# Graph network on one core: four transfers begun by GpSimd instead of ScalarE, and VectorE's gates, splits and low parts in another order

## The reference, cut to what matters

```python
for _ in range(5):
    s_in, s_out = state @ in_W.T + in_b, state @ out_W.T + out_b
    a = concatenate([A @ s_in, A.T @ s_out, state])
    r = sigmoid(a @ r_W.T + r_b)
    z = sigmoid(a @ z_W.T + z_b)
    h_hat = tanh(concatenate([a_in, a_out, r * state]) @ h_W.T + h_b)
    state = (1 - z) * state + z * h_hat
out = layernorm(x + tanh(state @ o1_W.T + o1_b) @ o2_W.T + o2_b)
```

## Time and profile before

| | us |
|---|---|
| median of 3 runs | 656.99 (656.04 to 657.47) |
| the profiled execution | 657.65 |
| its span, first to last instruction | 655.9 |
| mean granted TensorE clock | 0.996 |

### The profile page before, as it was taken

The page is one execution under the profiler, slowest core; times in us unless marked ns, Lnnn a source line. Parts: engine busy times, 40 slices in busy tenths (PEclk is TensorE's granted clock), DMA queues, the critical chain, the costliest instruction groups (busy, mean ns, idle before and its releaser), DMA issues. The chain is left out here.

```text
span 655.9 us, 8678 instructions
## 1 busy us (share of the span) xinstructions
PE 638.1 (97%) x2860; PEld 525.3 (80%) x2860; DVE 524.4 (80%) x833; ACT 418.2 (64%) x562; POOL 68.1 (10%) x61
## 2 busy tenths in 40 slices
PE   8999999999999999999999999999999999999993
PEld 7888888887888788788888877888887888887883
DVE  4996889799578739987896998887689888746886
ACT  2774645478357726895665688575758966674645
POOL 0092025200500720000000000000000000000012
PEclk9999999999999999999999999999999999999998
DMA  8999657213200270324034223403342250213003
GB/s 290 332 360 239 169 179 195 42 46 49 101 1 32 58 196 37 67 63 161 33 131 66 92 63 66 160 32 128 58 134 55 42 193 1 96 65 129 1 0 132
DMA packets 111609, 70.40 MB, mean 107 GB/s; under 512 B 89424, under 2 KB 95696, under 8 KB 110544
## 3 DMA queue, kind: packets, MB, share of 16 engines
q1 hardware_dynamic: 103056, 68.84, 35.1%
q10 hardware_dynamic: 8512, 1.05, 1.1%
HBM read 47.85 MB, written 19.40 MB: 103 GB/s over the span
## 5 line engine op out<-in xcount | busy, mean ns | idle before, releaser
L1158 ACT ACTIVATE work<-work,bias 128x512 f32<-128x512 f32 x120 | 86.0, 723 | 125.2 <-DVE work L1679 124.6
L1679 DVE SCALAR_TENSOR_TENSOR work<-degree,deg_w,bank 128x512 f32<-128x512 uint16 x120 | 88.4, 744 | 28.1 <-PE bank L703 27.3
L1017 ACT ACTIVATE ring<-a 128x1024 fp32r<-128x1024 uint8 (+1 forms) x91 | 91.7, 1048 | 6.3 <-PE bank L822 3.1
L701 PE MATMUL bank<-u_c,fold 128*128 128x512 f32 x240 | 94.1, 392 | 1.6 <-DVE work L1679 1.5
L702 PE MATMUL bank<-u_c,fold 128*128 128x512 f32 x240 | 93.4, 389 | 0.0
L703 PE MATMUL bank<-u_c,fold 128*128 128x512 f32 x240 | 93.4, 389 | 0.0
L822 PE MATMUL bank<-ring,rows 128*128 128x512 f32 x384 | 90.8, 390 | 0.3 <-DVE ring L1452 0.3
L714 PE MATMUL bank<-ring,rows 128*128 128x512 f32 x384 | 88.6, 389 | 0.2 <-issue 0.2
L1050 ACT ACTIVATE ring<-sums,minus 128x1024 fp32r<-128x1024 uint8 x72 | 80.3, 1139 | 7.5 <-PE bank L822 6.5
L822 PEld LDWEIGHTS bank<-ring,rows 128*128 128x128 f32 x384 | 71.7, 188 | 16.5 <-DVE ring L1452 1.0
L714 PEld LDWEIGHTS bank<-ring,rows 128*128 128x128 f32 x384 | 72.0, 188 | 15.5 <-issue 0.6
(11 more groups left out here) (168 smaller groups left out, 1110.9 us busy)
## 6 DMA issues: line engine op xcount, KB each, us to landing
sums<-sums_dram SPq DMA_DIRECT2D x12, 768.0 KB, 5.0
stage<-in_adj_dram SPq DMA_DIRECT2D x15, 512.0 KB, 8.6
sums<-in_adj_dram SPq DMA_DIRECT2D x13, 512.0 KB, 6.4
turned_dram<-work SPq DMA_DIRECT2D x12, 512.0 KB, 2.6
rows<-turned_dram SPq DMA_DIRECT2D x192, 32.0 KB, 2.0
sums_dram<-sums SPq DMA_DIRECT2D x4, 768.0 KB, 3.5
l_dram<-rs_c SPq DMA_DIRECT2D x3, 1024.0 KB, 3.9
rs_c<-l_dram SPq DMA_DIRECT2D x3, 1024.0 KB, 4.9
```

The lines of the kernel that those rows point to most:

```text
L701: nc.tensor.matmul(out_, wh, vh, start=first, stop=False)
L1017: nc.scalar.activation(out_, in_, ACT.Copy).then_inc(s, 1)
L1158: nc.scalar.activation(gates[:, g, e, :], gates[:, g, e, :], ACT.Tanh if g == H else ACT.Sigmoid, bias=bias[:, g, e:e + 1]).then_inc(gate_ ...
L1679: nc.vector.scalar_tensor_tensor(out=gates[:, g, e, :], in0=degree[:, c * CW:(c + 1) * CW], scalar=deg_w[:, g, e:e + 1], in1=g_bank[s % 3] ...
```

## The change

Six edits.

1. In the second chunk of a side VectorE reads gate 2 right behind gate 1, ahead of `rs(0)`, the turns, `rs_low(0)` and `rs(1)`. In the other chunks nothing moves.
2. For step 1 alone, the two `split_state` of each side leave the gate chunk before it and stand in `half_aggregate`, on ScalarE behind casts 13 and 15, on VectorE behind the first four tests of symmetry.
3. In `aggregate_pair`, side 0, the two `row_low(t, 1, h)` of VectorE stand behind the casts 2 and 3 and not ahead of them.
4. GpSimd's third `sum_blocks` waits for the mix W5 of the second side of step 1, and not for the states of the first.
5. The four transfers of chunk 3 that ScalarE began are begun by GpSimd, with a semaphore of their own (`rows_fourth`), for which every reader of these rows waits beside the old one.
6. The semaphore `zeroed` is folded into `const_ready`, whose last value is 9.

```diff
+            def turn_move(t):
+                k, n = NC - 1, NQ - 1
+                pool.wait_ge(turned, DB * NC * (t + 1))
+                for r in range(NQ):
+                    nc.gpsimd.dma_start(...).then_inc(rows_fourth, 16)
...
             pool.wait_ge(pair_stored, S_PAIR)
+            turn_move(0)
             pool.wait_ge(row_lo, row_count(1, (NC - 1, 1)))
             sum_blocks(1, range(6))
-            pool.wait_ge(state_new, S_TWO + 2 * TWO)
+            pool.wait_ge(mixed, mixed_at(1, 1, W5))
...
             sum_blocks(3, range(6))
+            for t in range(1, LAST):
+                turn_move(t)
...
@@ ScalarE, gate_chunk_two
-                if not ending:
+                if not ending and not half(t + (c == NC - 1)):
                     for e in range(DB):
                         split_state(*((t, 2) if c == 1 else (t + 1, 0)), e)
@@ ScalarE, half_aggregate
                 for k in range(10, 12):
                     if side == 0:
                         row_high(t, 2, k - 10)
-                        turn_move(t - 1, range(2 * (k - 10), 2 * (k - 9)))
                     cast(t, side, k)
                 for k in range(12, 16):
                     cast(t, side, k)
+                    if k % 2 == 1:
+                        split_state(t, 2 * side, k // 2 - 6)
@@ VectorE, gate_chunk
                     update(t, c - 1, first_gate=lambda: gate(t, c, 0))
                     next_pair(0)
                     gate(t, c, 1)
+                    gate(t, c, 2)
                     rs(t, c, 0)
...
-                gate(t, c, 2)
+                if not (c == NC - 1 or c == 1 and not first):
+                    gate(t, c, 2)
                 rs_low(t, c, 1)
...
-                if c == NC - 1 and not last or c == 1 and not first:
+                if (c == NC - 1 and not last or c == 1 and not first) and not half(t + (c == NC - 1)):
@@ VectorE, half_aggregate
                 for _ in range(4):
                     test()
+                for e in range(DB):
+                    split_state(t, 2 * side, e)
@@ VectorE, aggregate_pair
                 cast(t, side, 1)
                 if side == 0:
                     row_low(t, L1, 0)
-                    for h in range(2):
-                        row_low(t, 1, h)
...
                 cast(t, side, 3)
+                if side == 0:
+                    for h in range(2):
+                        row_low(t, 1, h)
```

More of the change, by code:

```diff
@@ L308, in fast_path @@
         fin_lo = sem("f_fin_lo")
-        zeroed = sem("f_zeroed")
         const_ready = sem("f_const_ready")
@@ L600, in _ @@
         def _(pool):
-            nc.gpsimd.memset(ident[:, :], 0.0).then_inc(zeroed, 1)
+            nc.gpsimd.memset(ident[:, :], 0.0).then_inc(const_ready, 1)
             nc.gpsimd.memset(ones[:, :], 1.0).then_inc(const_ready, 1)
@@ L608, in _ @@
                 nc.gpsimd.memset(minus[:, n:n + 1], -1.0 - n).then_inc(const_ready, 1)
-            pool.wait_ge(zeroed, 1)
+            pool.wait_ge(const_ready, 8)
             nc.gpsimd.affine_select(out=ident[:, :], in_=ident[:, :], compare_op=ALU.not_equal, fill=1.0,
@@ L630, in sum_bytes @@
                     n += level < len(TREE) - 1
+            def turn_move(t):
+                k, n = NC - 1, NQ - 1
+                pool.wait_ge(turned, DB * NC * (t + 1))
+                for r in range(NQ):
+                    nc.gpsimd.dma_start(rows[n * SQ:(n + 1) * SQ, LO, k * BC:(k + 1) * BC, :].bitcast(F32)
+                                        .rearrange("a b (e r d) -> a (b e) r d", e=DB, r=NQ)[:, :, r, :],
+                                        turned_T[r * SQ:(r + 1) * SQ, n].rearrange("p b e d -> p (b e) d")).then_inc(rows_fourth, 16)
             def sum_blocks(n_, some):
@@ L663, in _ @@
                 sum_bytes(c)
-            pool.wait_ge(const_ready, 8)
+            pool.wait_ge(const_ready, 9)
             pool.wait_ge(pair_ready, (NC - 1) * NP + 4)
@@ L987, in output @@
                         last.then_inc(o_done, 1)
-            pe.wait_ge(const_ready, 8)
+            pe.wait_ge(const_ready, 9)
             pe.wait_ge(ones_ready, 1)
@@ L1109, in split_state @@
                 high(st_c[:, HI, e, :], stateT[:, e, c * CW:(c + 1) * CW], st_hi)
[L1111 to L1119, removed]
             def row_high(t, k, h):
@@ L1144, in row_high @@
                     q, d = {L11: (2, 0), L21: (3, 0), L22: (3, 1)}[k]
-                    act.wait_ge(rows_loaded[q], 16 * NQ * NQ * t)
+                    if q == NC - 1:
+                        act.wait_ge(rows_fourth, 16 * NQ * t)
+                        act.wait_ge(rows_loaded[q], 16 * NQ * (NQ - 1) * t)
+                    else:
+                        act.wait_ge(rows_loaded[q], 16 * NQ * NQ * t)
                     high(rows[:, HI, q * BC:(q + 1) * BC, d * P:(d + 1) * P], rows[:, LO, q * BC:(q + 1) * BC, d * P:(d + 1) * P].bitcast(F32), row_hi)
@@ L1150, in row_high @@
                 else:
-                    act.wait_ge(rows_loaded[k], 16 * NQ * NQ * t)
+                    if k == NC - 1:
+                        act.wait_ge(rows_fourth, 16 * NQ * t)
+                        act.wait_ge(rows_loaded[k], 16 * NQ * (NQ - 1) * t)
+                    else:
+                        act.wait_ge(rows_loaded[k], 16 * NQ * NQ * t)
                     b = k * BC + 2 * h
@@ L1325, in aggregate_pair @@
                 cast(t, side, 8)
-                if side == 0:
-                    turn_move(t - 1, range(2))
                 cast(t, side, 9)
                 if side == 0:
-                    turn_move(t - 1, range(2, 4))
                     row_high(t, L1, 0)
@@ L1510, in l_add @@
                 if k == L2:
-                    dve.wait_ge(rows_loaded[3], 16 * NQ * NQ * t)
+                    dve.wait_ge(rows_fourth, 16 * NQ * t)
+                    dve.wait_ge(rows_loaded[3], 16 * NQ * (NQ - 1) * t)
                     dve.wait_ge(state_new, t * S_TWO)
```

3 lines of the change are left out of this document (2 added, 1 removed).

## The result

| | before | after |
|---|---|---|
| median, us | 657.12 (656.04 to 657.47, 4 runs) | 659.62 (659.42 to 660.28, 4 runs) |
| profiled execution, us | 657.65 | 659.42 |
| its span, us | 655.9 | 657.6 |
| mean granted clock | 0.996 | 0.995 |

Ratio of after to before: 1.0042, 95% interval 1.0027 to 1.0057. The change makes the kernel slower, by 1.8 to 3.7 us (the medians differ by 2.5, the ratio gives 2.8); 660.0 had been predicted, and slower with a chance of 0.80.

A forecast was written before the change was run, and what follows sets the result against it. TensorE, busy 638.1 of 655.9 us, was taken as the bound, with VectorE setting the end. Terms 1.5 + 1.4 + 2.4 - 0.6 - 1.2 - 0.7 = +2.8, rounded to 3: 656.99 + 3.0 = 660.0 us; 8-in-10 range 657.3 to 662.2.

The forecast's parts named there:

- A: Rival: fifth casts are in time, so early gate 2 costs only in the last chunk; 656.9 us, chance 0.12.
- B: Rival: reading gate 2 early frees TensorE and later work has slack enough; faster, 652.6 us, chance 0.08.
- C: Rival: the transfers begun by GpSimd are slow and readers wait; 668 us, or 664 if milder, chance 0.08.
- Part 1: Early gate 2, chunk 3 of steps 1 to 3: low part and fifth cast late, +0.5 us each, +1.5 us.
- Part 2: Early gate 2, chunk 1 of steps 2 to 4: fifth cast late, 0.45 us each, +1.4 us; step 1 free.
- Part 3: Early gate 2, last chunk of the last step: VectorE's queue stands still, gate 5 late, +2.4 us.
- Part 4: Splits out of the chunk before step 1's first side: fifth cast 0.6 us earlier, -0.6 us (ends 0 and -1.2).
- Part 5: GpSimd's third sum behind W5 in step 1: P5 casts no longer slowed, wait gone, -1.2 us.
- Part 6: Step 3, low parts behind casts 2 and 3: casts earlier, low parts with 0.2 us margin, -0.7 us.
- Part 7: Chunk 3's transfers begun by GpSimd: ScalarE's casts no earlier without them, no reader waits, 0 us.

The follow-up runs named there:

- e12: The changed kernel with VectorE's two low parts of the splits behind gate 5 in chunk 3 of steps 1 to 3; 657.67 us, ratio 1.0010.
- e9: e8 with gate 4 ahead of the two low parts of the split in chunk 3 of steps 1 to 3; 652.76 us, ratio 0.9935.
- e11: e8 with VectorE's two low parts of the splits behind gate 5 in chunk 3 of steps 1 to 3; 651.58 us, ratio 0.9919.
- e1: The changed kernel with gate 2 back in its old place behind rs(1) everywhere; 653.65 us, ratio 0.9943.
- e3: The kernel before with only gate 2 moved right behind gate 1 in the second chunk of each side; 664.15 us, ratio 1.0101.
- e2: The changed kernel with gate 2 in its old place in the last chunk of the last step alone; 657.40 us, ratio 1.0006.
- e7: The kernel before with only the splits of step 1's two sides moved into its aggregations; 655.58 us, ratio 0.9982.
- e6: The kernel before with only the low parts of row chunk 1 put behind casts 2 and 3; 655.81 us, ratio 0.9984.
- e10: e3 with chunk 3's four transfers begun by GpSimd instead of ScalarE, and `zeroed` folded into `const_ready`; 662.92 us, ratio 1.0094.
- e4: The changed kernel with chunk 3's four transfers begun by ScalarE again, on the new semaphore; 659.91 us, ratio 1.0041.
- e5: The kernel before with only GpSimd's third sum waiting for W5 of step 1's second side; 655.56 us, ratio 0.9984.
- e8: e1 with rs(1) and gate 2 ahead of rs_low(0) in chunk 3 of steps 0 to 3; 652.46 us, ratio 0.9929.

## Why the prediction was right, point by point

The predicted difference was +3.0 us; the ratio gives +2.8 (1.8 to 3.7). No rival came: A needed the fifth casts in time, B the low parts too, C slow transfers, and none of the three was so.

**Part 1 (+0.5 a chunk): right.** The wait for the low part took the place of the one for gate 2: 0.60, 0.48 and 0.44 us in steps 1 to 3 with the hidden 0.16, where 0.6 was predicted. From TensorE's first own matmul of h in chunk 2 to that in chunk 3 it took 16.96, 16.83 and 16.83 us where it had taken 17.00, 16.93 and 16.93, so the gain is 0.1 us or less. And the fifth cast was late: +0.56 and +0.55 in the two stretches where it stands alone. e12 shows that it is this cast. Its chain is gate 5, tanh, cast (e9, e11).

**Part 2 (+0.45 a chunk): right in size**, with +0.44, +0.47 and +0.63, but made of smaller pieces than I wrote; that they add up to the same is in part luck. I looked for one stall of 0.25 us of the matmuls. Steps 2 and 3 have none on the list of waits; only step 4 has (0.15 us of idle time). The weight loads show it. The weights are the rows, and the ring tile is the other factor, but TensorE's wait for the tile stands ahead of the load and the matmul alike, and so the load waits too, which elsewhere runs ahead of its matmul. In step 2 the fifth cast ends at 329.38 + 1.14 = 330.52, the load comes at 330.57, and from the second matmul of that tile on all are 0.11 us late, with 0.11 more at the next tile; some 0.1 more is lost at the own parts, whose low part is just in time.

```profile
329.38 2.18 ACT L1062 ACTIVATE ring<-sums,minus 128x1024 fp32r<-128x1024 uint8 x2
...
330.57 0.76 PEld L834 LDWEIGHTS bank<-ring,t_flat 128*128 128x128 f32 x4 [0.27 <-ACT ring L1062]
...
324.11 0.44 PE L713 MATMUL bank<-rs_c,own 128*128 128x512 f32 x1
```

Step 4 loses 0.2 more because I took step 2's rows for all three steps. In step 4 VectorE has a comparison of the symmetry test (L1621) between the second low part and gate 3, and everything behind it is later: the fifth cast ends at 565.47 + 1.14 = 566.61, which is 6.61 us behind the first own matmul (560.00), where it is 6.41 in step 2 (330.52 behind 324.11).

```profile
559.53 0.69 DVE L1621 SCALAR_TENSOR_TENSOR ident<-stage 128x512 uint8<-128x512 uint8 x1
...
565.47 2.18 ACT L1062 ACTIVATE ring<-sums,minus 128x1024 fp32r<-128x1024 uint8 x2
```

In step 1 chunk 1 costs 0.2 and not nothing (-1.06 against e1's -1.25), 0.11 of it at the own parts. That it is so little is owed to edit 2, which has taken the splits away: in e3, without edit 2, this stretch is 0.74 longer.

**Part 3 (+2.4): right**, +2.32, and e2 takes it away. The times counted through were 627.3 for ScalarE's last high parts, 629.2 for gate 3, 629.9 for the residual and 633.7 for gate 5; the trace has 627.33, 629.20, 629.86 and 633.56. A queue counted instruction by instruction, with each duration from a row, holds here to 0.15 us. That even the clock times agree is chance: the chunk begins where it did (its side's first own matmul of h at 603.63 us, before at 603.62), because gains and losses ahead of it had just cancelled.

**Part 4 (-0.6): right**, -0.55 with edit 1 and -1.20 without it (e1, e7): both of the numbers in its text, the value and the end of its range. The 0.65 between them is a cost of edit 1.

**Part 5 (-1.2): right**, -1.06 with edit 1, -1.27 alone. The P5 casts take 2.32 us for two where they took 4.29, since GpSimd's sum starts when they are over:

```profile
214.22 2.32 DVE L1460 TENSOR_TENSOR ring<-a 128x1024 fp32r<-128x1024 uint8 x2
...
219.35 1.42 POOL L656 TENSOR_TENSOR sums<-a,byte_one 128x512 uint32<-128x512 uint32 x1 [44.43 <-DVE work L1506]
```

**Part 6 (-0.7): right.** With part 1 in the same stretch -0.2 was forecast and -0.14 came; alone it is -0.68 (e6). In e1 it is -0.39. There the low parts begin 17.05 us behind TensorE's mark of the chunk and 16.73 in e6, and TensorE waits for them, since VectorE waited longer for the rows over DRAM (0.76 us, in e6 0.43). So the prediction's margin of 0.2 us was about right for the landing that it had read, and a later landing uses it up. What the prediction did not see is that parts 1 and 6 work on the same wait: e3 and e10, which have edit 1 and not edit 3, are no longer than before in this stretch (0.00 and -0.10), because TensorE, late by part 1, finds the P5 casts done. The sum of the two parts is right, but how much of it edit 3 brings in the changed kernel no run here tells: none takes edit 3 alone out of it.

```profile
391.09 0.69 DVE L1528 TENSOR_TENSOR work<-rows 128x512 f32<-128x512 f32 x1 [0.76 <-DMA rows<-turned_dram]
```

**Part 7 (0): the total right, the reason wrong.** I wrote that ScalarE's casts are no earlier without its transfers, from step 1, where that is so. In step 2 of a kernel whose ScalarE is late it is not: the issues hold two of its next instructions by 0.55 to 0.97 us (in the kernel before one, by 0.35), and the transfers' move saves 0.45 us in the trace beside the other edits (after against e4), 0.84 without them (e3 against e10). I took one step's rows for all four. Rival C's price was never paid: no reader of the last quarter waits for GpSimd, whose four issues in step 1 end at 157.21 us, SP's twelve at 161.83.

**The edits one by one and together.** Edits 1, 5 and 6 (e10) cost 6.0 us, edit 4 (e5) brings 1.05, edit 2 (e7) 1.03, edit 3 (e6) 1.1, each against its own runs of before. The sum is +2.8, what the ratio of the whole gives. That they add up so well is partly luck, and within the intervals: in the traces the same four give +3.5 from step 0 c2 to the last gate 5, and the whole +3.2. Edits 1 and 2 add up ahead of step 1 (+0.64 - 1.20, after -0.55), but in step 1 edit 2 spares edit 1 some 0.55 us (0.74 without it, 0.2 with it). The rest goes the other way in small pieces, 0.15 of it on the way to step 3 c0, where edits 1 and 3 work on the same wait (part 6).

## What to carry to other kernels

An engine that takes its instructions in order should do a read that frees a buffer when the buffer can be read, and not when the order is tidy: if the producer is far behind, everything written behind the read stands still with it (4.28 us here), and even where the read ends a wait of the bound engine, what was put back by it is the next wait. Before moving an instruction, count the queue through to the last thing that the bound engine takes from it, which here was ScalarE's cast behind the tanh of gate 5, and look for work with slack (the split's low parts, used 7 us later) that stands ahead of it: moving that brought 1.95 us in the changed kernel (e12) and 0.9 in e8 (e11). And read the cost of a DMA issue, and the margin of a cast, in every step, not in one.

## What was not expected of the hardware

**Some restarts cost 0.1 us that no list of waits of matmuls has.** They are to be seen in the rows of the weight loads (part 2: 0.27 us of idle time of the load, no idle time of the matmul, and 0.11 us lost).

**Issues of ScalarE can hold its own casts.** In e3, one transfer's issue took 1.51 us and two took 1.46, and ScalarE's next instruction came when the issue ended (280.95 behind 279.33 + 1.51). In e4, in the same place, one took 1.85. The first issue in each group took 0.61 to 0.65 us in all traces. In the step before, with the same twelve of SP in flight, the longest took 0.88 or 0.89. What lengthens them is open.

**GpSimd begins such transfers as fast as the others.** Four take 2.53 us, 0.6 us each, and land after 2.0 us in the median (the second block: tiles, queue, operation, count, KB each, us to landing), as SP's do; SP's twelve take 7.86 us in step 1 where they took 9.15.

```profile
154.68 2.53 POOL L637 DMA_DIRECT2D rows<-work  x4 [37.05 <-ACT ring L1029]
...
153.97 7.86 SPq L426 DMA_DIRECT2D rows<-work  x12
```

```profile
rows<-work SPq DMA_DIRECT2D x48, 32.0 KB, 2.0
...
rows<-work POOLq DMA_DIRECT2D x16, 32.0 KB, 2.0
```

The Trainium skill, page DMA: Bandwidth & Descriptors, section Anatomy of one DMA — SWDGE (gpsimd) path, has about 2 us for one; the 2.0 agree. The prediction's estimate from it of 8.3 us for four, one after the other, does not: they overlap, and are issued in 2.53 us. The starving behind VectorE that the page SBUF — State Buffer speaks of (section Who interferes with whom) did not show in these sixteen.

**GpSimd and VectorE slow each other in other places too.** GpSimd's sum takes 1.42 us beside the tests of symmetry (the row in part 5), where the same operation of the same sum, `sums<-a,byte_one`, took 1.04 in the kernel before; beside the P5 casts the sum of two tiles had taken 2.15 us. And edit 4 has moved the slowing, not ended it: the four tests beside the sums take 5.28 us where they take 4.08 in e7, which has edit 2 and not edit 4, and the two low parts of the split behind them 3.22 us and not 1.28. TensorE waited for none of it. The changed kernel and e7:

```profile
224.39 3.22 DVE L1450 TENSOR_TENSOR st_c<-stateT,st_c 128x512 fp32r<-128x512 f32 x2
...
224.29 1.28 DVE L1444 TENSOR_TENSOR st_c<-stateT,st_c 128x512 fp32r<-128x512 f32 x2
```
